# A transformer layer on eight cores: the first two groups' matmuls taken by turns, their second matmuls further behind, and the weight loads in another order

## The reference

```python
xn = layernorm(x)                                   # x: 16 x 2048 x 1024, f32
Q, K, V = xn @ Wq, xn @ Wk, xn @ Wv                 # 1024 -> 128
attn = softmax(causal(Q @ K.T * 128**-0.5)) @ V @ Wo
hidden = xn @ W1 + b1                               # 1024 -> 4096
imag = w_imag * sin(theta + 0.1 * hidden)
phase = cos(theta) * w_real + sin(theta) * w_imag
ffn = relu(hidden + phase * imag * 0.1) @ W2 + b2   # 4096 -> 1024
out = x + attn + ffn
```

## Time and profile before

| what | value |
|---|---|
| median of 3 runs | 1022.63 us |
| the profiled execution: its time, its span | 1024.46 us, 1022.9 us (core 2, the slowest) |
| spans of the 8 cores | 1016.6 to 1022.9 us |
| PE busy, share of the span | 994.5 us, 97% |
| DVE, ACT, POOL busy | 600.7, 396.7, 73.5 us |
| busy share of the DMA engines up to 125 us, and after it | about full; about a third |

### The profile page before, as it was taken

How to read it: one execution, slowest core, us unless ns; L and a number is a source line. 1 busy time by engine, 2 the same in 40 slices (tenths; PEclk the granted TensorE clock), 3 DMA queues, 4 the chain that set the end, 5 groups by cost and what they waited for, 6 DMA issues and landing times.

```text
span 1022.9 us, 20849 instructions; the slowest of 8 cores (1016.6 to 1022.9 us)
## 1 busy us (share of the span) xinstructions
PE 994.5 (97%) x7193; PEld 687.2 (67%) x7319; DVE 600.7 (59%) x1511; ACT 396.7 (39%) x742; POOL 73.5 (7%) x128
## 2 busy tenths in 40 slices
PE   6989999999999999999999999999999999999998
PEld 5656667666676766667666676766667676676765
DVE  4557566565666566665565655565566656655544
ACT  1435532344435344443333434344442434434221
POOL 4300010100001000010100001000010100000000
PEclk8989999999999999999999999999999999999999
DMA  7999944433415334163323416242342532414321
GB/s 151 176 174 184 167 81 126 103 65 93 96 63 128 88 79 81 63 134 94 95 45 97 88 63 121 81 102 43 112 82 81 119 82 77 99 42 103 102 44 42
DMA packets 85336, 98.85 MB, mean 97 GB/s; under 512 B 61552, under 2 KB 61680, under 8 KB 83952
## 3 DMA queue, kind: packets, MB, share of 16 engines
q1 hardware_dynamic: 76304, 62.80, 22.2%
q0 software_dynamic: 8640, 34.61, 20.6%
q10 hardware_dynamic: 288, 0.10, 0.1%
HBM read 84.02 MB, written 16.78 MB: 99 GB/s over the span
## 4 chain that ended last, share of the span: by engine, by line
PE 87%; DMA 5%; ACT 3%; issue 2%; DVE 2%; POOL 1%; DVEq 0%; ACTq 0%; POOLq 0%
PE psW L494 41%; PE psO L583 38%; DMA W_sb<-w 4%; PE psA L347 3%; PE psA L464 1%; PE psA L367 1%; PE psO L563 1%; PE psA L395 1%; DVE X L542 1%; DVE u L520 1%; ACT pr L419 1%; ACT L417 1%; ACT ss L514 1%; DMA X<-x 1%; ACT L422 0%
## 5 line engine op out<-in xcount | busy, mean ns | idle before, releaser
L494 PE MATMUL psW<-xn,W_sb 128*128 128x256 bf16 (+1 forms) x4112 | 526.1, 273 | 10.6 <-DMA W_sb<-w 6.0
L583 PE MATMUL psO<-W_sb,rb 128*128 128x512 bf16 x1936 | 488.3, 380 | 8.8 <-ACT rb L530 2.1
L494 PEld LDWEIGHTS psW<-xn,W_sb 128*128 128x128 bf16 x4112 | 399.9, 98 | 143.3 <-issue 14.7
L514 ACT ACTIVATE ss<-psW,ph_sb 128x256 bf16<-128x256 f32 x512 | 239.7, 474 | 575.7 <-PE psW L494 350.5
L520 DVE SCALAR_TENSOR_TENSOR u<-ss,Rp_sb,psW 128x256 f32<-128x256 bf16 x512 | 245.5, 480 | 316.4 <-ACT ss L514 315.4
L583 PEld LDWEIGHTS psO<-W_sb,rb 128*128 128x128 bf16 x2048 | 198.7, 98 | 172.0 <-issue 7.5
L534 DVE TENSOR_SCALAR rb<-u,fp_sb 128x256 bf16<-128x256 f32 x504 | 177.0, 351 | 46.6 <-DVE u L520 21.6
L542 DVE TENSOR_TENSOR X<-psO,X 128x512 f32<-128x512 f32 x96 | 59.5, 681 | 2.9 <-PE psO L583 2.9
L702 POOL DMA_DIRECT2D X<-b2rep x32 | 30.1, 950 | 293.2 <-DMA X<-x 285.6
L293 POOL TENSOR_SCALAR rs<-mv 128x1 f32<-128x1 f32 x32 | 7.6, 238 | 594.7 <-DVE mv L291 553.0
L406 DVE TENSOR_SCALAR_CACHE_REDUCE lg<-psA 128x512 f32<-128x512 f32 (+2 forms) x80 | 48.3, 603 | 0.0
(11 more groups left out here) (56 smaller groups left out, 247.2 us busy)
## 6 DMA issues: line engine op xcount, KB each, us to landing
X<-x SPq DMA_DIRECT2D x60, 512.0 KB, 4.7
X<-b2rep POOLq DMA_DIRECT2D x32, 512.0 KB, 5.6
out<-X SPq DMA_DIRECT2D x64, 256.0 KB, 2.3
W_sb<-w POOLq DMA_DIRECT2D x10, 1024.0 KB, 68.7
W_sb<-w POOLq DMA_DIRECT2D x8, 512.0 KB, 18.0
W_sb<-w POOLq DMA_DIRECT2D x8, 256.0 KB, 11.8
Wqkv_sb<-wqkv POOLq DMA_DIRECT2D x1, 768.0 KB, 28.1
pT<-pr SPq DMA_TRANSPOSE x26, 3.5
```

The costliest lines, as they stand in the source:

```text
L494: fn = lambda e, k=k: e.matmul(psW[u % 2][:, at:at + n], w1_block(c, k), xg[:, k * GT + at:k * GT + at + n], start=(k == 0), stop=(k == NC ...
L514: t_sin[u] = act.mark(lambda e: e.activation(ss[u % 2][:], psW[u % 2][:, 0:GT], AF.Sin, scale=0.1, bias=ph_sb[:, c:c + 1]))
L583: fn = lambda e, i=i, tt=tt, h=h, u=u, c=c: e.matmul(psO[i][:], rb[u % NRB][:, tt * 128:(tt + 1) * 128], W2_sb[:, c * D + h * 512:c * D + ...
```

## The change

1. The units of slots 0 to 63 are no longer in the order of the passes: first blocks 0 to 4 of group 0, and then a block of group 1 and a block of group 0 by turns. The f2 go in the order of the passes still (`turns`), and the passes are others, of equal blocks in both groups.
2. The lag of the f2 is 10 slots at first and falls by one in five slots from slot 36 on (`usual_lag`), to 5.
3. The first six units write six banks (psW and psO) and six buffers of sines.
4. W1 and W2 are loaded in another order, in 15 pieces, and POOL issues the first four pieces of W1 as soon as the angles are computed, without waiting for a tile of x. The four x tiles are issued at once.
5. More idle work: 140 at the start, 8 and 10 around the transposes, 8 in each of slots 1 to 4. The constants come over SP's queue. 16 units rather than 8 may use ACT for the relu, every second one of them. `wo_share` and `add_b2` of groups 0 and 1 are hung on turns, not on slots.

```diff
-WARM = 100
-RELU_ACT = 8
-PIECES = (1, 1, 1, 1, 2, 2, 2, 2, 4, 4, 4, 4, 4)
+WARM = 140
+RELU_ACT = 16
+HEAD = 5
+NWIDE = 6
+PIECES = (1, 1, 1, 1, 1, 1, 2, 2, 2, 2, 2, 4, 4, 4, 4)
...
-        load_x(0, 0)
-        load_x(1, 1)
-        load_x(2, 2, t_x[1])
-        load_x(3, 3)
+        for tile in range(4):
+            load_x(tile, tile)
...
-        pool.after(t_x[0])
-        load_w1(0)
-        load_w1(1)
...
-        passes = [(0, 0, 3), (1, 0, 5), (0, 3, 9), (1, 5, 12), (0, 9, 16),
-                  (1, 12, 20), (0, 16, 25), (1, 20, 29), (0, 25, 32), (1, 29, 32)]
+        passes = [(0, 0, 5), (1, 0, 5), (0, 5, 10), (1, 5, 10), (0, 10, 17),
+                  (1, 10, 17), (0, 17, 25), (1, 17, 25), (0, 25, 32), (1, 25, 32)]
...
+        units = [(0, c) for c in range(HEAD)]
+        for c in range(NCF):
+            units.append((1, c))
+            if c + HEAD < NCF:
+                units.append((0, c + HEAD))
+        units += [(g, c) for g in range(2, NG) for c in range(NCF)]
...
+        turns = [(unit_of[g, c], c == a, c == b - 1, b == NCF)
                  for g, a, b in passes for c in range(a, b)]
...
+            bank = wide[u] if u < NWIDE else psW[u % 2]
+            sines = wide_ss[u] if u < NWIDE else ss[u % 2][:]
+
+            old = u - NWIDE if u < NWIDE + 2 else u - 2
+            pe.after(t_w1[PIECE_OF[c]], t_xn[g, 0], t_xn[g, 1], t_stt.get(old))
...
+        def usual_lag(slot):
+            return max(LAG, min(10, 10 - (slot - 36) // 5))
...
+        for p in (7, -1, -2, -3, -4, 8, 9):
+            load_w1(p) if p > 0 else load_w2(-p)
+        t_wqkv = l_wqkv.start(pool, lambda e: e.dma_start(Wqkv_sb[:], wqkv))
+        for p in (-5, -6, 10, -7, 11):
+            load_w1(p) if p > 0 else load_w2(-p)
+        t_wo = l_wo.start(pool, lambda e: e.dma_start(Wo_sb[:], wo))
+        for p in (-8, -9, -10, 12, -11, 13, -12, 14, -13, -14):
+            load_w1(p) if p > 0 else load_w2(-p)
...
+                ns = [nxt] if nxt < end - 2 else list(range(nxt, end + 1))
+                if len(ns) > 1 and slot < end + min(3, lag.get(slot, LAG)):
                     break
-        assert nxt == NU and not plan
+                assert all(turns[n][0] < slot for n in ns)
+                f2(ns)
+                nxt = ns[-1] + 1
+        assert nxt == NU and not plan and not after_turn
```

More of the change, by code:

```diff
@@ L220, in idle_work @@
             for _ in range(n):
-                pe.do(lambda e: e.matmul(psW[1][:, 0:128], diag[:], diag[:], start=True,
+                pe.do(lambda e: e.matmul(psO[3][:, 0:128], diag[:], diag[:], start=True,
                                          stop=True, skip_group_check=True))
@@ L363, in vv @@
             xg = xn[xn_buf[g]]
-            pe.after(*wqkv_token, free)
+            pe.after(t_wqkv, free)
             for tt in range(2):
@@ L520, in f1, with on_act @@
             t_stt[u] = dve.mark(lambda e: e.scalar_tensor_tensor(
-                u2[u % 2][:], ss[u % 2][:], Rp_sb[:, c:c + 1],
-                psW[u % 2][:, 0:GT], ALU.mult, ALU.add))
+                u2[u % 2][:], sines, Rp_sb[:, c:c + 1],
+                bank[:, 0:GT], ALU.mult, ALU.add))
+        def on_act(u):
+            return 0 <= u < RELU_ACT and u % 2 == 0
         def relu(u):
-            if u in t_relu:
-                return
             c = units[u][1]
-            if u < RELU_ACT:
-                act.after(t_stt[u])
+            i, free = rb_free.pop(0)
+            rb_of[u] = rb[i]
+            if on_act(u):
+                act.after(t_stt[u], free)
                 t_relu[u] = act.mark(lambda e: e.activation(
[L531 to L536, removed]
+                    rb_of[u][:], u2[u % 2][:], AF.Relu, bias=b1c[:, c:c + 1]))
+            else:
+                dve.after(t_stt[u], free)
+                t_relu[u] = dve.mark(lambda e: e.tensor_scalar(
+                    rb_of[u][:], u2[u % 2][:], b1c[:, c:c + 1], 0.0,
+                    ALU.add, ALU.max))
+            rb_ix[u] = i
         def evict(g, i, done, final):
@@ L579, in f2 @@
                 if first:
-                    pe.after(bank_out[i])
+                    pe.after(bank_out[i] if ns[0] else t_stt.get(2 + i))
                 for u in us:
@@ L600, in f2 @@
             for u in us:
-                t_f2[u] = done
+                rb_free.append((rb_ix[u], done))
+            for fn in after_turn.pop(ns[-1], []):
+                fn()
         plan = {}
+        after_turn = {}
         def at(slot, fn):
@@ L661, in plan_tile @@
             at(p0, lambda: weighted(J))
-            lag[e0 + 2] = lag[e0 + 3] = 3
-            lag[e0 + 4] = lag[e0 + 5] = 4
+            for slot, less in ((2, 2), (3, 2), (4, 1), (5, 1)):
+                lag[e0 + slot] = usual_lag(e0 + slot) - less
         def plan_att(g):
@@ L775, in build_nc @@
         plan_tile(5, 48, 54, 58, 62)
-        at(43, lambda: wo_share(0))
-        at(52, lambda: wo_share(1))
-        for slot in range(13):
-            lag[slot] = 1 if slot < 3 else 2
+        for slot in range(64):
+            lag.setdefault(slot, usual_lag(slot))
         for g in range(2, NG):
```

121 lines of the change are left out of this document (48 added, 73 removed).

## The result

The changed kernel takes 1030.05 us (median of 4 runs, 1029.34 to 1030.41), the kernel before 1022.58 us beside it (4 runs, 1021.72 to 1022.70): a ratio of 1.0074, interval 1.0057 to 1.0091, so 7.5 us slower, where 4.9 us were forecast. The profiled execution of after took 1030.41 us, with a span of 1028.9 us; before it was 1024.46 and 1022.9.

A forecast was written before the change was run, and what follows sets the result against it. The prediction took PE as the bound, except up to 58.90 us, where the weight stream binds. It summed +2.0 (later landing) and +2.9 (clock) to +4.9 us: 1022.63 + 4.9 = 1027.5, range 1021.0 to 1031.0 for 8 in 10.

The forecast's parts named there:

- the likeliest case: Slot 34's late landing and the clock loss behind it both cost time, together +2.1 to +8 us; chance 0.62.
- The deciding wait: In slot 34 three f2 wait 4 to 7 us for piece 11 of W2, with 48 blocks landed.
- The landing: The 48th block, for slot 34, lands at 94.1: 96.2 - 3.1 (earlier stream) + 1.0 (seventh x tile).
- the term +2.0: Slot 34's landing at 94.1 is 2.0 us later than 92.1, the group start that keeps step with the kernel before.
- The clock: Behind slot 34's wait the granted clock falls, charged at +2.9 us; at least 0 if it holds.
- Rival 1: Behind slot 34's wait the clock holds or loses little, leaving +2.0 us: 1024.6; chance 0.12.
- Waits near 60: PE waits about 2 to 3 us near 60 us for piece 7.
- The other parts, at nothing: Everything before slot 34, such as idle work, banks and relus on ACT, ends in its wait and costs nothing.
- all later work is the same set of matmuls in a similar order: After slot 34, a group of f2 starting at 92.1 keeps step with the kernel before.
- A difference carries over: The +4.9 us reckoned on the profiled execution (1024.46) is added to the median, 1022.63, giving 1027.5.
- Rival 2: Later blocks take 1.5 us, not 1.63; the 48th lands 4 us earlier, at 90.1: 1020.6; chance 0.22.
- Rival 3: Up to the 48th block, four more pieces leave gaps, 9.6 us on top of the forecast: 1037.1; chance 0.04.

The follow-up runs named there:

- experiment two: The changed kernel with passes ending at block 16, so slot 34's f2 group does not need piece 11 of W2: 1029.8 us, ratio 1.0060 to the kernel before.
- the cut pieces: The changed kernel with two loads exchanged, plus the pieces of blocks 20 to 23 cut into 1, 1 and 2 blocks: 1024.45 us, ratio 1.0015.
- the relu experiment: The changed kernel with two loads exchanged, plus pass-end groups of three f2 at least two slots behind their last unit: 1027.09 us, ratio 1.0040.

## Why the prediction was right, and where it was off

It held in sign, in place and within its range; the likeliest case was the one that happened.

- **The deciding wait** was the one named: slot 34, piece 11 of W2, a group of f2 into psO. PE was through with the f1 there at 88.2 (87.35 + 0.87), within the 87.4 to 90.3 forecast; the wait was 5.91 (forecast 4 to 7). Over the eight cores it was 2.9 to 5.9. The exchange of two loads shows what it was worth: -5.2 us.
- **The landing** was forecast at 94.1 and came at 93.8, and the work began at 94.29: the term +2.0 measured +2.2. Its parts were a sum of estimates (-3.1 for the start, +1.0 for the x tile, now issued at 86.6 and not at 94.7) that came out well together, in part by luck: the early start alone moved the wait near 55 by 3.7 us on the slowest cores and by 2.2 on the mean of the eight, and the stretch in the middle was never tested by itself. Over the cores the landing's wait ended between 91.5 and 94.3, on the mean at 92.9.
- **The clock**: forecast +2.9, measured +2.55 on core 6; it fell on all eight, where the group of f2 is shown with 4.4 to 5.2 us as against 2.75. Rival 1 fell for this kernel. But the step "that is longer than the wait behind which the clock fell" was a weak reason, since the length alone doesn't decide (below).
- **Waits near 60**: forecast 2 to 3 us, found 3.16 at 60.96 on core 6. Real work starts at 14.5, a little ahead of the 15 to 16 forecast.
- **"The other parts, at nothing"** was right ahead of slot 34, all of which the wait swallowed, and wrong behind it. The step that failed is "all later work is the same set of matmuls in a similar order": the same set it is, but the new pass ends put groups of f2 right behind their relu, and that gave +1.0 us on core 6 and +0.7 to +1.0 on the others, with 0.3 more unassigned. I had looked for later waits on landings alone; experiment two shows that the waits for DVE behind 100 us can be 4 us dearer than before with other pass ends (7.1 against 2.8).
- **"A difference carries over"** failed by 1.5 us. The two profiled executions differ by 1030.41 - 1024.46 = 5.95 and the medians by 7.5: before's profiled execution was 1.9 above its median of 1022.58, after's only 0.4. I said how it stood to the median, and then treated the offset as common to both.
- **What I didn't see**: that the cores of before were uneven for a reason which the change removes. The forecast was worked on the two slowest cores only; on core 1, the fastest, the wait near 55 ended 5.2 us earlier than on core 2, so the early loads had next to nothing to give it, and it lost 9.6 us, from 1016.6 to 1026.2.
- **Rival 2**, a faster stream that gains, had the right mechanism for one part: the early start alone gains 3.7 us. It was not faster by smaller gaps in the middle, as I worked it out, but at the start. (Its sum has a slip: from 1.63 to 1.5 us a block is 0.13 and not 0.1, so 40 blocks give 5.2 us, not 4; nothing above rests on it.) **Rival 3**, gaps between small pieces, didn't happen: the last piece of W2 landed at 125.0 us on the mean of the eight cores with 26 pieces of W1 and W2 (the early start), at 124.6 with 30 (after) and at 124.7 with 34 (the cut pieces). The rule of the Trainium skill (DMA: Bandwidth & Descriptors, Rules for kernel authors) to make each DMA 1 MiB or more isn't borne out for pieces that stand queued behind others. The 2.0 us that the prediction takes from the same page stand in its section Anatomy of one DMA.

## What to carry to other kernels

While a stream of loads is the bound, write down for each wait the number of blocks that must have landed and the work done by then; what decides is the wait where the two are furthest apart, and exchanging two loads ahead of it was worth 5.2 us here. Test the parts of a large change alone: here one part was worth -3.7 us and was buried under 11. And do the sum on the fastest core as well as on the slowest, for a change of the start may only even them out.

## What the runs showed of the hardware that was not expected

- **Whether the clock fell behind a wait was not set by the wait's length.** It held behind 3.30 us (core 6 of the early start, above), 3.35 us (core 7 there), 3.16 us (after, near 61) and 2.34 us (the exchange). It fell behind 2.51 us (core 4 of the early start), behind 2.21 us (60 idle matmuls) and on some cores behind 1.59 us (evict wait of the relu experiment, where on core 0 ten f2 matmuls behind it took 3.87 us, 2.16 at full speed). So it can't be charged at a wait with certainty. What else decides, these runs don't separate.
- **How long it stood low differed between the cores.** By windows of 1 us, at the long wait of each core: in before 6.8 us on cores 0 and 2, the two slowest, and 3.4 us on the other six; in after 6.8 us on seven cores and 3.4 us on core 2, the fastest; with the early start 3.4 us on four cores and none on four. What it costs is half of what of that stretch lies behind the wait: on core 2 of after it began as the wait ended, at 91.5, and was over by 95.0, so 1.7 us; on core 6 it began at about 93.1 and was over by 99.9, so 5.6 us of it lay behind the wait, 2.8 us by this reckoning and 2.55 by the timeline.
- **A queued piece cost nothing that shows**: the end of the stream did not move with four or eight pieces more (the numbers stand under rival 3).
- **With the loads issued early the cores came out even.** With the x tiles one behind the other and W1 behind the first, the wait near 55 ended over a stretch of 5.2 us; with all issued at once, over 1.9 us, and the spans of the cores of one execution lay 3.0 us apart on average, where it was 6.0. Which of the two waits was the one that mattered, the run does not separate.
